# A two-layer network of gated attention and experts: block ends without Pool's drain, the second experts' first inputs prepared in the attention before, and rows gathered by halves

## The chip, the cores and the metric

The kernel runs on one core of a Trainium2 chip. The engines of the core are called TensorE (PE in the rows; its loading of weights is PEld), VectorE (DVE), ScalarE (ACT), Pool (GpSimd) and SyncE (SP), and a q behind an engine's name is the sequencer that reads its instructions. The metric is the device time of one execution in microseconds, as a median of several. The profile is one execution that the hardware profiler took, and its rows count from the start of that execution's span.

## What is computed

Two layers, each a gated cross attention and a gated mixture of experts, on x of 8 x 512 tokens with 256 values. The change touches the seams between the parts, and above all the last part:

```
x = x + tanh(g_xattn[0]) * attention0(layernorm(x), ctx)    # 16 heads, causal
x = x + tanh(g_ffn[0])   * experts0(layernorm(x))           # 32 experts, 8 for each token
x = x + tanh(g_xattn[1]) * attention1(layernorm(x), ctx)    # 16 heads, masked
x = x + tanh(g_ffn[1])   * experts1(layernorm(x))           # 8 experts, 2 for each token
...
E, K, H = (8, 2, 1024)                                      # experts1; T = 4096 tokens
cap = int(K * CAP_FACTOR * ((T + E - 1) // E))              # 1024 places in each expert
logits = xt @ wg
gates_k, idx_k = jax.lax.top_k(softmax(logits), K)          # then divided by their sum
h = jax.nn.relu(jnp.einsum('ecd,edh->ech', disp, w1) + b1[:, None, :])
out = jnp.einsum('ech,ehd->ecd', h, w2) + b2[:, None, :]
y = jnp.einsum('tk,tkd->td', gates_k * valid, out[idx_k, loc_c])
```

Here `disp` holds for each expert the rows of up to 1024 tokens that chose it, in order; places that stay empty give nothing.

## The kernel before

Four stages follow one another, each written as a block in which every engine has its own list of instructions: the first attention, the first experts (`experts0`, 32 experts), the second attention and the second experts (`experts1`, 8 experts). A function `attention` serves both attentions; its tiles belong to an object `Layer`. A block ends at a barrier of all engines. In a block as `nc.Block()` makes it, Pool executes a drain ahead of that barrier (at the line of the function that has the block: 334 in `attention`, 1233 in `experts0`). Behind the block its semaphores are given back: `Semaphores.__exit__` (lines 69 and 70) clears them and adds a barrier of its own. This clearing is built as a second drain of Pool, a clear of the range of semaphores, and then the barrier of line 70.

The second attention works through 8 batches in a software pipeline (`ITERATIONS` from -3 to B + 1). For each batch it ends with the routing: VectorE counts in `base` how many tokens have gone to each expert and makes the places `idx`, and Pool scatters the tokens' rows (the values after the norm, the token's number, the gates) to `rows` in main memory (line 1192). After the last batch VectorE copies the counts to `tot0` (line 1150). SyncE loads and stores around it: `stack` (line 474), the residual `xres` (458), the stores of the new x (488).

`experts1` (line 1490) goes over the 8 experts with `pipeline`: a prologue for expert 0, then one iteration for each expert, `iteration(cur, nxt)`, which also begins the next expert's work. `par` is the expert's parity; most tiles stand twice. Each expert has 1024 rows in 8 tiles of 128:

- Before the first expert VectorE makes the indices of all the experts' rows, `gidx`, from `tot0` in four operations (lines 1638 to 1643: `late`, `gfl`, `gfl`, `gidx`). For each expert `pick` copies its 8 columns to `gidx_e` (1652) and its first bias to `b1_e` (1655); for expert 0 it waits for the biases between the two.
- Pool's `gather` waits for the pick, and for the transposes that last read the buffer `row[par]`, and issues 8 indirect DMAs of 128 rows (1715). They all count up one semaphore for each parity. `add` (1723) issues 8 indirect DMAs that add the finished rows into x.
- TensorE's `turn` (1549 to 1557) transposes four tiles of one half of the columns into the bank `e_x_bank`; four turns make an expert. ScalarE copies the bank to `xT` (1609), and the next turn waits for that copy, since there is one bank. Turn k is column half k // 2 and token half k % 2; turn 0 waits for all 8 gathers.
- `up` (1559 to 1571) is the first product, 16 matmuls for each half of the tokens (block 0 and block 1), into four banks `e_h_bank`, which ScalarE and VectorE empty in turn with bias and relu (1618, 1673). Block 0 waits for the weights and for all four copies of the expert.
- `down` (1575 to 1588) is the second product, four groups of 16 matmuls for a pair of blocks; in block 0 the four turns of the next expert stand behind each 8 of them.
- SyncE loads each expert's `w1` and `w2` (1535, 1536), those of expert 0 at the start of the block, the two biases `b1`, `b2` (1523, 1524) behind the first gathers, and at the end copies x to the output.

Of the kernel before, what the change touches and what calls it, by code (L numbers as in the profile page):

```python
# [13 lines left out]
P = 128  # L14
# [247 lines left out]
class Layer:  # L262


    def __init__(self, c, ctx, layer):
        t_ = lambda name, shape, dt=F32: sb(c, ctx, f"{name}_{layer}", shape, dt)
        sem = lambda n: ctx.enter_context(c.nc.semaphore(f"{n}_{layer}"))
        rows = STACK + (6 if layer == 0 else 3)
# [4 lines left out]
        self.qst = [t_(f"qst{i}", [rows, HEADS, S], BF16) for i in range(2)]  # L273
        self.kst = [t_(f"kst{i}", [rows, HEADS, S], BF16) for i in range(2)]
        self.va = [t_(f"va{i}", [P, NT, HEADS, 32]) for i in range(3)]
        self.m3T = [t_(f"m3T{i}", [3 * HEADS // 2, S], BF16) for i in range(2)]
        if layer:
            self.mask3 = t_("mask3", [P, B * S], BF16)
            self.maskc = t_("maskc", [P, B * NT])
        self.w_in, self.b_in, self.l_in, self.stack_ones, self.w_ones, self.w_t, self.w_put, self.zeroed = (  # L280
# [25 lines left out]
def attention(c, layer, a, x_in, ctx_in, mask, wq, bq, wk, bk, wv, bv, wp, bp, wroute, x_out, rows,  # L306
              qk_dram, mask_dram, tot0=None, token=None):
# [26 lines left out]
    with ExitStack() as ctx:  # L334
# [57 lines left out]
        if layer == 0:  # L392
# [13 lines left out]
                 "hchain", "lo_rdy", "lchain")  # L406
# [5 lines left out]
        block = ctx.enter_context(nc.Block())  # L412
# [33 lines left out]
        def _(sp):  # L446
# [68 lines left out]
            for it in ITERATIONS:  # L515
# [349 lines left out]
        def _(dve):  # L865
# [282 lines left out]
            if tot0 is not None:  # L1148
                dve.wait_ge(evac["rank"], B)
                dve.tensor_copy(tot0[:, :], base[:, 0, :]).then_inc(s["ochain"], 1)  # L1150
# [74 lines left out]
def experts0(c, table, gate_up, down, x, token, a, mask, wq, bq, wk, bk, wv, bv, wp, bp, wroute):  # L1225
# [7 lines left out]
    with ExitStack() as ctx:  # L1233
# [28 lines left out]
        block = ctx.enter_context(nc.Block())  # L1262
# [227 lines left out]
def experts1(c, rows, w1, b1, w2, b2, x, tot0, out):  # L1490
# [4 lines left out]
    with ExitStack() as ctx:  # L1495
        t_ = lambda name, shape, dt=F32: sb(c, ctx, f"e1_{name}", shape, dt)
        two = lambda name, shape, dt=F32: [t_(f"{name}{i}", shape, dt) for i in range(2)]
        names = ("rows_in0", "rows_in1", "weights_in0", "weights_in1", "bias_in", "x_full", "x_evac",
# [3 lines left out]
        rows_in, weights_in = (s["rows_in0"], s["rows_in1"]), (s["weights_in0"], s["weights_in1"])  # L1502
# [3 lines left out]
        h = two("h", [P, HC, HALF])  # L1506
        y = two("y", [P, TILES, D])
        b1_s, b2_s = t_("b1", [P, E1, HC]), t_("b2", [P, E1, D])
        b1_e = two("b1_e", [P, HC])
        gidx = t_("gidx", [P, E1, TILES], U32)  # L1510
        gfl, late = t_("gfl", [P, E1, TILES]), t_("late", [P, E1, TILES])
# [9 lines left out]
        def _(sp):  # L1521
            def biases():
                sp.dma_start(b1_s[:, :, :], b1.rearrange("e (c p) -> p e c", p=P), allow_slow_non_contiguous=True).then_inc(s["bias_in"], 16)
# [257 lines left out]
```

## Time and profile before

| | us |
|---|---|
| median of three runs | 2087.16 (2085.93 to 2091.36) |
| the profiled execution | 2089.91 |
| its span | 2088.2 |
| first attention, in the span | 0 to 652 |
| first experts | 652 to 899 |
| second attention | 899 to 1576 |
| second experts | 1576 to 2072 |
| copy of x to the output | 2072 to 2088 |

The limits of the stages are the barriers, to the nearest microsecond. The rows below are of two kinds. Views such as the busy time or the windows give sums over a stretch; a timeline gives single instructions, or runs of equal ones. In a timeline row the number in brackets is the time for which the engine had stood idle just before, and behind the arrow is what ended that: an engine and its line, a DMA, or "issue", when the profile shows nothing. PEclk is the granted clock of TensorE as a share of 2.4 GHz. The drains are instructions of Pool's sequencer and don't count as busy time of Pool.

### The profile page before, as it was taken

How to read it: one execution, taken by the hardware profiler on the slowest of the kernel's cores; microseconds unless marked ns; L12 is line 12 of the kernel's file. 1: busy time of each engine (PE TensorE's matmuls, PEld its weight loads, DVE VectorE, ACT ScalarE, POOL GpSimd, SP SyncE). 2: the span in 40 equal slices, each digit the busy share in tenths (PEclk: the TensorE clock that was granted, in tenths of full speed). 3: DMA queues.
4: the chain of work that ended last, by engine and by line, in shares of the span. 5: the costliest groups of instructions: out<-in, count | busy, mean ns of one | idle time of the engine just before them, and what ended most of it. 6: DMA issues, size and time to landing. Idle time of an engine off the chain costs nothing. (4 is left out here: it accounts for less than half of the span.)

```text
span 2088.2 us, 29804 instructions
## 1 busy us (share of the span) xinstructions
PE 1779.8 (85%) x10491; PEld 1063.2 (51%) x10491; DVE 1070.1 (51%) x2740; ACT 888.4 (43%) x1684; POOL 605.0 (29%) x580
## 2 busy tenths in 40 slices
PE   3799898989864988737999999999954999999995
PEld 1456555555544877613344444443322666666664
DVE  4556877787745644306877777778321112121121
ACT  3366565655531222222777787766721111111110
POOL 4212211120002777622221233211132233333322
PEclk9999999999976999967999999999976999999998
DMA  3545445334224778625323432431114133333314
GB/s 114 167 121 173 151 137 169 107 121 134 75 74 117 172 164 171 114 75 164 102 67 114 132 119 77 126 110 58 42 47 132 30 78 81 81 76 76 81 20 101
DMA packets 204243, 222.84 MB, mean 107 GB/s; under 512 B 33438, under 2 KB 195231, under 8 KB 203431
## 3 DMA queue, kind: packets, MB, share of 16 engines
q1 hardware_dynamic: 176458, 177.48, 27.7%
q0 software_dynamic: 27648, 43.60, 11.1%
q8 instruction: 78, 1.28, 0.3%
q14 instruction: 59, 0.48, 0.1%
HBM read 155.06 MB, written 86.93 MB: 116 GB/s over the span
## 5 line engine op out<-in xcount | busy, mean ns | idle before, releaser
L889 DVE TENSOR_REDUCE nmx<-mxb 128x1 f32<-128x512 f32 (+1 forms) x896 | 521.7, 608 | 244.0 <-PE mxb L660 147.8
L747 ACT ACTIVATE pt<-stb 128x512 f32<-128x512 f32 x832 | 475.3, 598 | 280.5 <-PE stb L680 155.9
L660 PE MATMUL mxb<-kst,qst 96*128 96x512 bf16 (+4 forms) x1024 | 335.9, 350 | 36.9 <-DVE nmx L889 27.2
L677 PE MATMUL stb<-qst,kst 99*128 99x512 bf16 (+4 forms) x1024 | 327.6, 345 | 8.2 <-DMA qst<-m3T 4.3
L1569 PE MATMUL e_h_bank<-e_xT,e_w 128*128 128x512 f32 x512 | 224.7, 597 | 6.1 <-ACT e_xT L1609 5.4
L1583 PE MATMUL e_y_bank<-e_w,e_h 128*128 128x256 f32 x1024 | 227.0, 379 | 0.0
L693 PE MATMUL ob<-pt,va 128*32 128x512 f32 (+3 forms) x2048 | 220.3, 525 | 2.7 <-ACT pt L747 1.7
L1583 PEld LDWEIGHTS e_y_bank<-e_w,e_h 128*128 128x128 f32 x1024 | 193.0, 190 | 31.7 <-issue 7.2
L677 PEld LDWEIGHTS stb<-qst,kst 102*128 102x128 bf16 (+1 forms) x1024 | 99.5, 99 | 213.3 <-ACT pt L747 136.0
L1171 POOL TENSOR_TENSOR qk<-qk,parts 128x512 f32<-128x512 f32 x64 | 73.0, 1161 | 436.4 <-ACT qk L782 227.8
L1723 POOL DMA_INDIRECT x_after_l<-e_y,e_token x64 | 99.5, 1555 | 282.0 <-DVE e_y L1688 267.3
L660 PEld LDWEIGHTS mxb<-kst,qst 99*128 99x128 bf16 (+1 forms) x1024 | 101.2, 99 | 151.3 <-DVE nmx L889 79.8
L1569 PEld LDWEIGHTS e_h_bank<-e_xT,e_w 128*128 128x128 f32 x512 | 97.3, 191 | 124.8 <-issue 124.2
L1618 ACT ACTIVATE e_h<-e_h_bank,e_b_e 128x512 f32<-128x512 f32 x64 | 44.0, 687 | 269.3 <-PE e_h_bank L1569 269.3
L1673 DVE TENSOR_SCALAR e_h<-e_h_bank,e_b_e 128x512 f32<-128x512 f32 x64 | 48.0, 750 | 171.1 <-PE e_h_bank L1569 171.1
L1684 DVE TENSOR_TENSOR e_y<-e_y_bank,e_b 128x512 f32<-128x512 f32 x32 | 22.1, 691 | 201.8 <-PE e_y_bank L1583 201.8
L1476 POOL DMA_INDIRECT x_after_l<-e_y,token x64 | 102.3, 1598 | 47.5 <-DMA x_after_l<-e_y,token 21.5
L663 PE MATMUL mxb<-hide_max,identb 128*128 128x128 bf16 x512 | 110.9, 223 | 0.0
L680 PE MATMUL stb<-hide_st,identb 128*128 128x128 bf16 x512 | 109.4, 221 | 0.0
L1177 POOL TENSOR_TENSOR parts<-qk,parts 128x512 bf16<-128x512 f32 x64 | 73.0, 1161 | 101.4 <-ACT parts L815 101.4
L1192 POOL DMA_INDIRECT rows<-rowb,idx x64 | 63.8, 997 | 114.3 <-DVE idx L1016 97.2
L1338 PE MATMUL e_bank<-e_xT,e_guT 128*128 128x256 f32 x384 | 88.6, 380 | 2.8 <-DVE e_h L1396 2.8
(242 smaller groups left out, 2514.7 us busy)
## 6 DMA issues: line engine op xcount, KB each, us to landing
qk_parts<-parts SPq DMA_DIRECT2D x16, 1536.0 KB, 6.2
qst<-qk_parts SPq DMA_DIRECT2D x384, 64.0 KB, 2.3
kst<-qk_parts SPq DMA_DIRECT2D x384, 64.0 KB, 2.3
e_w<-in_L_ffn_w SPq DMA_DIRECT2D x16, 1024.0 KB, 7.4
rows<-rows SPq DMA_DIRECT2D x15, 1060.0 KB, 8.7
crow<-in_ctx SPq DMA_DIRECT2D x16, 512.0 KB, 3.9
x_after_l<-xres SPq DMA_DIRECT2D x16, 512.0 KB, 3.3
e_gu_nat<-in_L_ffn_gate_up_proj SPq DMA_DIRECT2D x64, 128.0 KB
```

Source lines behind the costliest of these rows:

```text
L660: last = pe.matmul(out, qst[par][0:rows_used, h, qt * P:(qt + 1) * P], kst[par][0:rows_used, h, 0:nk], start=True, stop=not causal)
L663: last = pe.matmul(out[:, nk - P:nk], c.identb[:, :], c.hide_max[:, :], start=False, stop=True)
L677: last = pe.matmul(bank[:, to:to + S - q_from(kt)], kst[par][0:ROWS, h, kt * P:(kt + 1) * P], qst[par][0:ROWS, h, q_from(kt):S], start=Tru ...
L680: last = pe.matmul(bank[:, to:to + P], c.identb[:, :], c.hide_st[:, :], start=False, stop=True)
L693: last = pe.matmul(ob[32 * j:32 * j + 32, q_from(kt):S], va[b % 3][:, kt, 4 * g + j, :], weights_of(b, g, kt, j), start=kt == 0, stop=kt = ...
L747: act.activation(pt[:, slot(b, u), q0:S], stb[no % N_ST][:, q0:S], ACT.Exp, scale=SCALE).then_inc(s["st_free"], 1)
L889: last = dve.tensor_reduce(nmx[:, qt, h:h + 1], got[:, at:at + k_to(qt)], AX.X, ALU.max, negate=True)
L1338: last = pe.matmul(out, guT[par][:, ci, q, :], xT[par][:, ci, :], start=ci == 0, stop=ci == NC - 1)
L1476: pool.indirect_dma_start(x, bass.IndirectOffsetOnAxis(token[:, TILES * e + i:TILES * e + i + 1], 0), y[e % 3][:, i, :], None, bounds_chec ...
L1569: last = pe.matmul(hb[q % 4][:, :], w1_s[par][:, ci, k * P:(k + 1) * P], xT[par][:, ci, blk * HALF:(blk + 1) * HALF], start=ci == 0, stop= ...
L1583: last = pe.matmul(yb[t][:, i * D:(i + 1) * D], h[blk][:, k, (2 * t + i) * P:(2 * t + i + 1) * P], w2_s[par][:, k, :], start=k == 0, stop= ...
L1723: pool.indirect_dma_start(x, bass.IndirectOffsetOnAxis(token[par][:, i:i + 1], 0), y[par][:, i, :], None, bounds_check=T + SPARE - 1, oob_ ...
```

## The change

*Block ends.* The block of `attention`, and with it both attentions, and that of `experts0` are made with `no_gpsimd_drain=True`. The block of `experts1` stays as it was, and so does `Semaphores.__exit__`.

*Weights and biases.* Tiles of the second attention that are no longer read get a second use: `qst[0]` holds expert 0's `w1` and `w2`, `kst[0]` the biases `b1` and `b2`, and `qst[1]` and `kst[1]` the hidden values `h` of the two blocks. SyncE loads the first four in the attention (a new line 554, in the iteration of the last batch), and waits for them at the end of that block. At the start of `experts1` it loads expert 1's weights, where it loaded expert 0's.

*Indices.* The four operations that make `gidx` stand at the end of VectorE's attention, behind the copy to `tot0`.

*Halves.* The gathers of an expert count up two semaphores, one for each four tiles. Turn k is now column half k % 2 and token half k // 2, and each pair of turns waits for its own four gathers. Block 0 of `up` waits for two copies, block 1 for four. In the prologue two turns and block 0 of `up` stand ahead of the other two turns. ScalarE's and VectorE's lists follow: ScalarE copies twice, empties block 0's banks and copies twice more; VectorE's `gates`, which needs all 8 gathers, stands behind its part of block 0.

The diff, cut to its core:

```diff
-        block = ctx.enter_context(nc.Block())
+        block = ctx.enter_context(nc.Block(no_gpsimd_drain=True))
...
+                if ffn and cur == B - 1:
+                    sp.wait_ge(s["st_full"], N_SCORE * (B - 1))
+                    for src, dst in zip(ffn, (a.w1, a.w2, a.b1, a.b2)):
+                        sp.dma_start(dst, src, allow_slow_non_contiguous=True).then_inc(s["ffn_in"], 16)
...
+            if ffn:
+                sp.wait_ge(s["ffn_in"], 64)
             sp.wait_ge(s["x_out"], 16 * B)
...
-        w1_s, w2_s = two("w1", [P, NC, F1]), two("w2", [P, HC, D])
+        w1_s, w2_s = [a.w1, t_("w1", [P, NC, F1])], [a.w2, t_("w2", [P, HC, D])]
...
             def first(n):
-                load(n)
-                sp.wait_ge(rows_in[0], 16 * TILES)
-                biases()
+                pass
...
             def turn(n, k):
-                par, cc, hf = n[1], k // 2, k % 2
-                if k == 0:
-                    pe.wait_ge(rows_in[par], n[0] * (16 * TILES) + 16 * TILES)
+                par, cc, hf = n[1], k % 2, k // 2
+                if cc == 0:
+                    pe.wait_ge(rows_in[par][hf], n[0] * HALF_IN + HALF_IN)
...
                 if k0 == 0 and blk == 0:
-                    pe.wait_ge(weights_in[par], b[0] * 32 + 32)
-                    pe.wait_ge(s["x_evac"], at(4, b, 4))
+                    wait(pe, weights_in[par], b[0] * 32 + 32 * par)
+                if k0 == 0:
+                    pe.wait_ge(s["x_evac"], at(4, b, 2 * blk + 2))
...
             def prologue(n):
-                for k in range(4):
+                for k in range(2):
                     turn(n, k)
                 up(n, 0, 0, HC)
+                for k in range(2, 4):
+                    turn(n, k)
...
-                                            bounds_check=2 * SLOTS - 1, oob_is_err=True).then_inc(rows_in[par], 16)
+                                            bounds_check=2 * SLOTS - 1, oob_is_err=True).then_inc(rows_in[par][2 * i // TILES], 16)
```

How the order of instructions moves is shown at three places. The first is TensorE at the start of `experts1`, before: `e_row` are the gathered rows, `e_x_bank` the transposes' bank, `e_h_bank` and `e_y_bank` the banks of the first and the second product.

```order
L1556 MATMUL e_x_bank<-ident,e_row 128x128 x16
L1569 MATMUL e_h_bank<-e_xT,e_w 128x512 x32
L1583 MATMUL e_y_bank<-e_w,e_h 128x256 x8
L1556 MATMUL e_x_bank<-ident,e_row 128x128 x4
L1583 MATMUL e_y_bank<-e_w,e_h 128x256 x8
L1556 MATMUL e_x_bank<-ident,e_row 128x128 x4
L1583 MATMUL e_y_bank<-e_w,e_h 128x256 x8
```

And now, where `qst_1` is the attention's tile that holds expert 0's weights and the hidden values:

```order
L1571 MATMUL e_x_bank<-ident,e_row 128x128 x8
L1585 MATMUL e_h_bank<-e_xT,qst_1 128x512 x16
L1571 MATMUL e_x_bank<-ident,e_row 128x128 x8
L1585 MATMUL e_h_bank<-e_xT,qst_1 128x512 x16
L1599 MATMUL e_y_bank<-qst_1 128x256 x8
L1571 MATMUL e_x_bank<-ident,e_row 128x128 x4
L1599 MATMUL e_y_bank<-qst_1 128x256 x8
L1571 MATMUL e_x_bank<-ident,e_row 128x128 x4
```

Of the 16 transposes that stood ahead of all matmuls, 8 have moved between block 0 and block 1 of the first product; the alternation with the second product, from there on, is as it was.

The second place is SyncE from the end of the second attention into `experts1`, before: `x_after_l` is x in main memory, `e_w` and `e_b` the tiles of weights and biases.

```order
L488 DMA x_after_l<-xres 128x4x256
L458 DMA xres<-x_after_l 128x4x256
L488 DMA x_after_l<-xres 128x4x256
L334 UNCONDITIONAL_BRANCH
L1520 UNCONDITIONAL_BRANCH
L1535 DMA e_w<-in_L_ffn_w 128x2x1024
L1536 DMA e_w<-in_L_ffn_w 128x8x256
L1523 DMA e_b<-in_L_ffn_b 128x64x1
L1524 DMA e_b<-in_L_ffn_b 128x2048
L1535 DMA e_w<-in_L_ffn_w 128x2x1024
L1536 DMA e_w<-in_L_ffn_w 128x8x256
```

And now:

```order
L495 DMA x_after_l<-xres 128x4x256
L465 DMA xres<-x_after_l 128x4x256
L554 DMA qst_1<-in_L_ffn_w 128x2x1024
L554 DMA qst_1<-in_L_ffn_w 128x8x256
L554 DMA kst_1<-in_L_ffn_b 128x64x1
L554 DMA kst_1<-in_L_ffn_b 128x2048
L495 DMA x_after_l<-xres 128x4x256
L341 UNCONDITIONAL_BRANCH
L1541 UNCONDITIONAL_BRANCH
L1550 DMA e_w<-in_L_ffn_w 128x2x1024
L1551 DMA e_w<-in_L_ffn_w 128x8x256
```

Expert 0's weights and the biases have moved ahead of the last store of the attention, and expert 1's weights stand where expert 0's stood.

The third is VectorE at the same seam, before: `tot` are the counts, `slot_in` and `slot_at` constant tables.

```order
L1150 COPY tot<-base 128x8
L334 UNCONDITIONAL_BRANCH
L1634 UNCONDITIONAL_BRANCH
L1638 TENSOR_TENSOR e_late<-slot_in,tot 128x64
L1639 TENSOR_SCALAR e_gfl<-tot 128x64
L1641 TENSOR_TENSOR e_gfl<-e_gfl,e_late 128x64
L1643 TENSOR_TENSOR e_gidx<-e_gfl,slot_at 128x64
L1652 COPY e_gidx_e<-e_gidx 128x8
L1655 COPY e_b_e<-e_b 128x8
L1662 CAST e_token<-e_row 128x8
```

And now:

```order
L1163 COPY tot<-base 128x8
L1166 TENSOR_TENSOR late<-slot_in,tot 128x64
L1167 TENSOR_SCALAR gfl<-tot 128x64
L1169 TENSOR_TENSOR gfl<-gfl,late 128x64
L1171 TENSOR_TENSOR gidx<-gfl,slot_at 128x64
L341 UNCONDITIONAL_BRANCH
L1654 UNCONDITIONAL_BRANCH
L1664 COPY e_gidx_e<-gidx 128x8
L1665 COPY e_b_e<-kst_1 128x8
L1684 TENSOR_SCALAR qst_1<-e_h_bank,e_b_e 128x512 x4
```

The four operations on the indices have moved ahead of the block's end, so that the pick of expert 0's indices, `e_gidx_e`, is the first that VectorE does in `experts1`.

## Rows read from the trace of the kernel before

**Rows 1.** Section 1 of the page: busy time, share of the span, instructions.

```profile
PE 1779.8 (85%) x10491; PEld 1063.2 (51%) x10491; DVE 1070.1 (51%) x2740; ACT 888.4 (43%) x1684; POOL 605.0 (29%) x580
```

**Rows 2.** TensorE timeline, 1589 to 1700: start, us, line, operation, count, [idle before].

```profile
1590.23 1.12 PE L1556 MATMUL e_x_bank<-ident,e_row 128*128 128x128 f32 x4 [35.44 <-DMA e_row<-rows,e_gidx_e]
...
1593.84 1.11 PE L1556 MATMUL e_x_bank<-ident,e_row 128*128 128x128 f32 x4 [0.69 <-ACT e_xT L1609]
...
1597.53 29.45 PE L1569 MATMUL e_h_bank<-e_xT,e_w 128*128 128x512 f32 x64 [0.78 <-ACT e_xT L1609]
...
1643.28 13.97 PE L1569 MATMUL e_h_bank<-e_xT,e_w 128*128 128x512 f32 x32 [0.73 <-issue]
```

**Rows 3.** Timeline of Pool, 1540 to 1605.

```profile
1577.98 1.10 POOL L1715 DMA_INDIRECT e_row<-rows,e_gidx_e  x1 [10.29 <-DVE e_gidx_e L1652]
...
1582.04 1.01 POOL L1715 DMA_INDIRECT e_row<-rows,e_gidx_e  x1 [0.30 <-issue]
...
1587.30 1.01 POOL L1715 DMA_INDIRECT e_row<-rows,e_gidx_e  x1 [0.31 <-issue]
```

**Rows 4.** Timeline of VectorE, 1540 to 1605.

```profile
1576.09 0.23 DVE L1638 TENSOR_TENSOR e_late<-slot_in,tot 128x64 f32<-128x64 f32 x1 [19.10 <-PEq L70]
...
1576.97 0.17 DVE L1652 COPY e_gidx_e<-e_gidx 128x8 uint32<-128x8 uint32 x1
```

**Rows 5.** Gathers issued in 1577 to 1579, then in 1581.8 to 1583.

```profile
DMA to landing us min/median/max: 6.3/6.3/6.3
...
DMA to landing us min/median/max: 3.4/3.4/3.4
```

**Rows 6.** Lines 334, 1233, 69: instruction, count, ns least/median/most, from to; idle.

```profile
L334 POOLq DRAIN  x2: 306/2795/5284, 622.9 to 1569.6; - x2
...
L1233 POOLq DRAIN  x1: 4137/4137/4137, 895.0 to 895.0; - x1
...
L69 POOLq DRAIN  x3: 98/173/174, 651.6 to 1575.0; - x3
```

**Rows 7.** Timeline of TensorE, 1655 to 2075.

```profile
1689.48 3.62 PE L1583 MATMUL e_y_bank<-e_w,e_h 128*128 128x256 f32 x16
1692.94 0.60 PE L1556 MATMUL e_x_bank<-ident,e_row 128*128 128x128 f32 x4
...
1700.72 0.60 PE L1556 MATMUL e_x_bank<-ident,e_row 128*128 128x128 f32 x4
1702.09 14.00 PE L1569 MATMUL e_h_bank<-e_xT,e_w 128*128 128x512 f32 x32 [0.76 <-ACT e_xT L1609]
...
1743.47 3.62 PE L1583 MATMUL e_y_bank<-e_w,e_h 128*128 128x256 f32 x16
1747.79 0.66 PE L1556 MATMUL e_x_bank<-ident,e_row 128*128 128x128 f32 x4 [0.71 <-DMA e_row<-rows,e_gidx_e]
1748.29 3.62 PE L1583 MATMUL e_y_bank<-e_w,e_h 128*128 128x256 f32 x16
```

**Rows 8.** Waits of TensorE, 1605 to 2030: us in sum, count, us of one.

```profile
PE e_h_bank L1569 <- ACT e_xT L1609: 4.6, 6, 0.8
PE e_x_bank L1556 <- DMA e_row<-rows,e_gidx_e: 4.4, 6, 0.8
```

**Rows 9.** Windows: us, busy PE, PEld, DVE, ACT, POOL; clock, DMA share, GB/s.

```profile
1508.00:1539.00 31.00, 25.80 (x177) 12.75 (x173) 7.73 (x43) 17.24 (x34) 7.89 (x8) 0.94 0.15 53
...
1597.00:1601.00 4.00, 3.47 (x4) 1.52 (x5) 0.38 (x3) 0.39 (x1) 0.00 (x0) 0.50 0.99 393
...
1997.00:2065.00 68.00, 68.00 (x255) 48.08 (x253) 12.54 (x23) 5.50 (x8) 18.45 (x12) 1.00 0.20 23
```

**Rows 10.** Timeline of SyncE, 1475 to 1600.

```profile
1507.90 0.37 SPq L458 DMA_DIRECT2D xres<-x_after_l  x1
1539.06 0.36 SPq L488 DMA_DIRECT2D x_after_l<-xres  x1
...
1590.61 4.68 SPq L1524 DMA_DIRECT2D e_b<-in_L_ffn_b  x1
```

More of the change, by code:

```diff
@@ L272, in __init__ @@
         self.wr = t_("wr", [P, NC, (E0, E1)[layer]])
-        self.qst = [t_(f"qst{i}", [rows, HEADS, S], BF16) for i in range(2)]
-        self.kst = [t_(f"kst{i}", [rows, HEADS, S], BF16) for i in range(2)]
+        self.qst = [t_(f"qst{i}", [P, HEADS, S], BF16) for i in range(2)]
+        self.kst = [t_(f"kst{i}", [P, HEADS, S], BF16) for i in range(2)]
         self.va = [t_(f"va{i}", [P, NT, HEADS, 32]) for i in range(3)]
@@ L1486, in _, with experts1 @@
                 pool.wait_ge(added[i], 16 * TILES * (E0 // 2))
-def experts1(c, rows, w1, b1, w2, b2, x, tot0, out):
+def experts1(c, a, rows, w1, w2, x, out):
     nc = c.nc
@@ L1620, in prologue @@
             def prologue(n):
-                for k in range(4):
+                for k in range(2):
                     evac(n, k)
                 hidden(n, 0, (0, 2, 4, 6))
+                for k in range(2, 4):
+                    evac(n, k)
             def iteration(cur, nxt):
@@ L1635, in _, with pick @@
         def _(dve):
-            full = tot0[:, :].unsqueeze(2).to_broadcast([P, E1, TILES])
-            dve.tensor_tensor(late[:, :, :], c.slot_in[:, :, :], full, ALU.is_ge).then_inc(s["ichain"], 1)
-            dve.tensor_scalar(gfl[:, :, :], full, -1.0, float(SLOTS), ALU.mult, ALU.add).then_inc(s["ichain"], 1)
-            dve.wait_ge(s["ichain"], 2)
-            dve.tensor_tensor(gfl[:, :, :], gfl[:, :, :], late[:, :, :], ALU.mult).then_inc(s["ichain"], 1)
-            dve.wait_ge(s["ichain"], 3)
-            dve.tensor_tensor(gidx[:, :, :], gfl[:, :, :], c.slot_at[:, :, :], ALU.add).then_inc(s["ichain"], 1)
-            dve.wait_ge(s["ichain"], 4)
-            def pick(n, first=False):
+            def pick(n):
                 par = n[1]
                 e = n[0] * 2 + n[1]
-                wait(dve, s["rows_in" + str(par)], n[0] * (16 * TILES))
+                for half in rows_in[par]:
+                    wait(dve, half, n[0] * HALF_IN)
                 wait(dve, s["act_h"], at(8, n, -8))
                 dve.tensor_copy(gidx_e[par][:, :].unsqueeze(1), gidx[:, bass.ds(e, 1), :]).then_inc(s["picked"], 1)
-                if first:
-                    dve.wait_ge(s["bias_in"], 32)
                 dve.tensor_copy(b1_e[par][:, :].unsqueeze(1), b1_s[:, bass.ds(e, 1), :]).then_inc(s["small"], 1)
@@ L1659, in gates @@
                 e = n[0] * 2 + n[1]
-                dve.wait_ge(rows_in[par], n[0] * (16 * TILES) + 16 * TILES)
+                for half in rows_in[par]:
+                    dve.wait_ge(half, n[0] * HALF_IN + HALF_IN)
                 wait(dve, s["added"], at(16 * TILES, n, -16 * TILES))
@@ L1690, in prologue @@
             def prologue(n):
-                pick(n, True)
+                pick(n)
+                hidden(n, 0, (1, 3, 5, 7))
                 gates(n)
-                hidden(n, 0, (1, 3, 5, 7))
             def iteration(cur, nxt):
```

50 lines of the change are left out of this document (32 added, 18 removed).

## The prediction

> **What bounds the kernel now.** I read the busy shares first: TensorE is busy for 85% of the span, no other engine for more than 51% [rows 1]. A mean over unlike stages prices nothing, so I went to the stretch that the change touches, the end of the second attention and the second experts, about 1557 to 2088 us, a quarter of the time.
>
> At its start TensorE stands for 35.44 us: its last work of the attention ends at 1554.79 (1590.23 less 35.44), the first transposes of the experts begin at 1590.23, and the row names the gathered rows as what ended the wait [rows 2]. Pool's and VectorE's timelines divide this hole: VectorE gets going at 1576.09, after a barrier [rows 4]; Pool issues the first gather at 1577.98, the fourth at 1582.04, the eighth and last at 1587.30 [rows 3]. What stands before the barrier are Pool's drains: the one that ends the attention starts at 1569.6 and takes 5.284 us, that of the first experts 4.137 us [rows 6].
>
> Behind the hole TensorE is the bound: from 1997 to 2065 it is busy 68.00 of 68 us at a granted clock of 1.00, that is 2.4 GHz [rows 9]. Before that it stops twice in each round: six waits on the gathered rows, 4.4 us in sum, and six on ScalarE's copy of the transposed rows, 4.6 us [rows 8]. One round is 58.81 us (1689.48 to 1748.29) [rows 7].
>
> **The change, part by part.**
>
> *Indices.* Four VectorE operations stood between the barrier and the pick of the first indices, from 1576.09 to 1576.97 [rows 4]: 0.88 us on the path, since Pool waits for that pick. They now follow the copy of the counts, which ends VectorE's attention at 1556.99 (1576.09 less 19.10 of idle) [rows 4], while the block ends with Pool at 1574.9 (1569.6 + 5.284) [rows 6]. Some 18 us cover them; without cover they would cost the 0.88 again.
>
> *Gathers by halves.* TensorE needs only the first four gathers to begin. The fourth started at 1582.04 and landed 3.4 us later [rows 3, 5], so at 1585.44, against 1590.23 for all eight: 4.79 us. Issued 0.88 earlier it gains 5.67 if the landing moves too. But the first gather took 6.3 us to land where the fourth took 3.4 [rows 5]: both land right behind the weight loads that SP issues at the same moment, and it still issues as many bytes there, now those of expert 1. I take 5.2, between the ends 4.79 and 5.67. The other four gathers now lie beside the first half's matmuls; these take over 13 us [rows 7], the gathers 5.3 us (1582.04 to 1587.30) and a landing.
>
> *Transposes.* Before the first large matmul stood four groups of transposes, each with ScalarE's copy behind it; now two. The latter two cost 3.69 us there (1593.84 to 1597.53), at half clock [rows 2]. They come back between the two runs of matmuls, at full clock: 0.60 us of matmuls [rows 7] and 0.69 of waiting for the copy [rows 2], twice, 2.6 us. Gain 1.1, and 0 if the clock is still low there. It was granted at 0.50 until about 1601, some 3.5 us into the dense matmuls [rows 9], so it should be up; I take 1.0. The half-speed stretch itself is neither gained nor lost: it follows the start of dense work, which only comes earlier.
>
> *The two waits of a round.* The first half is awaited alone at the first transposes, and it was issued 5.3 us earlier than the last gather, for a wait of 0.71 [rows 7]: the wait goes. Transposes now go by halves of the tokens, so a new expert's first matmuls need the first two copies, done some 7 us before, and not the fourth: this wait goes too. Prices are taken start to start, since a wait also breaks the overlap of neighbouring matmuls. Rows: from the second product's group at 1743.47 to the transposes at 1747.79 are 4.32 us, against 3.46 without a wait (1689.48 to 1692.94), so 0.86. Copy: from the last transposes at 1700.72 to the matmuls at 1702.09 are 1.37, against 0.50 (1747.79 to 1748.29), so 0.87 [rows 7]. Six rounds have the first, seven changes of expert the second: 5.2 + 6.1 = 11.3 us. By the idle times alone it would be 9.7 (4.4 + 4.6, and the 0.73 of the first change, which is listed as issue) [rows 2, 8]. What is late next is TensorE itself; the gathers' first half has over 4 us to spare.
>
> *Weights and biases in the attention.* Four loads join SP's queue behind the last load of the residual, 1507.90, and ahead of the last store, 1539.06; nothing of SP lies between [rows 10]. Issuing them takes some 6 us, of which the broadcast of a bias 4.68 [rows 10]. Their 3.1 MB need 8 us at the 393 GB/s of 1597 to 1601, and the DMA engines have a share of 0.15 from 1508 to 1539 [rows 9]. Nothing in the experts waited for the first expert's weights, so nothing is gained either: 0. Were the cover gone, the last store would slip, and only the block's end waits for that.
>
> *Ends without a drain.* Pool's drain ahead of the barrier goes at two places that matter, 5.284 and 4.137 us [rows 6]. But the semaphores are still cleared behind the barrier, and that begins with a drain of Pool (line 69), and all engines wait for it at the next barrier. Today it takes 98 to 174 ns [rows 6], because the other has just been paid. The drain's length follows from what Pool did before: 306 ns behind plain arithmetic, 4 to 5 us behind indirect DMAs [rows 6]. So the second drain should take over the wait of the first. Ends: 0, and 9.4 us if the time belongs to the removed instruction. I take 0.2 us a place for the short drain that merges, 0.4.
>
> The Trainium skill ("Perfetto Trace Analysis", section "Sequencer-only Instruction (DRAIN, etc)") lists a drain as sequencer work with two actors, the sequencer and the semaphores. By that the time would go with the instruction, which is the first rival below. The rows speak against it with a spread of 306 to 5284 ns.
>
> **Sum.** 5.2 + 1.0 + 11.3 + 0.4 = 17.9 us (the 0.88 is inside the 5.2). The profiled execution took 2089.91 us, 2.75 above the median of 2087.16, and becomes 2072.0; the median becomes **2069.3**.
>
> **Rivals.**
> - *The drains really go.* The rest as above and 9.0 us more (9.4 less the 0.4 counted): 2060.3. For it: the drain at line 69 has never been seen paying. Against it: 306 ns where no DMA stood before. Chance 0.12.
> - *Another wait takes the place of the two in the round*, say the banks of the first product, so that a round stays at 58.8 us: only 6.6 remain, 2080.6. Against it: where rows came early, at the first change, TensorE ran on without any row wait. Chance 0.06.
> - *The halves do not do what they say*: the fourth gather is held behind expert 1's weights until the eighth is nearly there. Then 5.2 shrinks to nothing: 2074.5. Against it the 3.4 us. Chance 0.03.
> - *Slower: the clock falls.* With both gaps gone TensorE streams through the loop, some 400 us, and if the clock were then granted at 1.2 GHz for part of it, each us at that level gives half a us back. It decides from 36 us on; 50 us would give 2094. Against it: 68 us without any gap at 1.00 [rows 9]. Chance 0.02.
> - The forecast itself: 0.77.
>
> **How the numbers follow.** The forecast's own span: the least gain is 4.8 + 0 + 9.7 + 0 = 14.5 (2072.7), the most 5.7 + 1.1 + 12.0 + 0.6 = 19.4 (2067.8), where 12.0 and 0.6 add a tenth of a us to each of the thirteen waits and to each barrier; with two us for the scatter of single runs 2066 to 2075. The drains' case must lie inside to keep what is left out under 2 in 10, so the range is 2058 to 2075. A measurement of this kernel tells 0.3% from no change, 6.3 us: faster means below 2080.9. Forecast, drains, halves and half of the second rival: 0.95 faster, 0.03 the same, 0.02 slower.
>
> **What would show it.** Right: TensorE's hole of 35.4 us becomes about 30; two groups of transposes, 16 matmuls, two groups, 16 matmuls; the list of waits for TensorE in the loop is nearly empty, a round is about 57 us; line 69's drain takes 4 to 5 us. Drains gone: it stays at 0.17 and VectorE starts the second experts near 1570.7. Wrong: a round still near 58.8, a granted clock under 1.00 in the loop, or a first half that lands later than 1585.5 counted from the same barrier.

## The result, and the profile after

The changed kernel takes 2055.18 us (four runs, 2052.29 to 2058.18) beside 2086.55 for the kernel before (four runs): a ratio of 0.9862, with a 95% interval of 0.9843 to 0.9882. The forecast of 2069.3 promised a gain of 18 us and the range ended at 2058; the gain is 31 us in this comparison, and two more comparisons further down give 0.9860 and 0.9885. The direction was right, the size was not. Line numbers below are those of the kernel that is named; the changed one has 1571, 1585 and 1599 where the kernel before has 1556, 1569 and 1583.

The first view is the timeline of TensorE in the changed kernel from 1540 to 1620, the answer to [rows 2] (start, us, line, operation, count, idle before and what ended it):

```profile
1570.52 1.11 PE L1571 MATMUL e_x_bank<-ident,e_row 128*128 128x128 f32 x4 [26.21 <-DMA e_row<-rows,e_gidx_e]
...
1574.12 16.82 PE L1585 MATMUL e_h_bank<-e_xT,qst 128*128 128x512 f32 x32 [0.69 <-ACT e_xT L1627]
1590.78 0.60 PE L1571 MATMUL e_x_bank<-ident,e_row 128*128 128x128 f32 x4
...
1593.41 14.00 PE L1585 MATMUL e_h_bank<-e_xT,qst 128*128 128x512 f32 x32 [0.69 <-ACT e_xT L1627]
1607.24 3.62 PE L1599 MATMUL e_y_bank<-qst 128*128 128x256 f32 x16
```

The hole ahead of the first transposes is 26.21 us, where it was 35.44, and the prediction said about 30. Behind it stand two groups of transposes, 32 matmul records (16 matmuls; each is recorded twice, as before), two groups, 32 records: the order that was forecast. TensorE's list of waits from 1605 to 2000 is empty, where [rows 8] had twelve. The rounds are seen in the timeline from 1655 to 1725, the answer to [rows 7]:

```profile
1664.09 3.62 PE L1599 MATMUL e_y_bank<-e_w,qst 128*128 128x256 f32 x16
1667.55 0.60 PE L1571 MATMUL e_x_bank<-ident,e_row 128*128 128x128 f32 x4
1667.98 3.62 PE L1599 MATMUL e_y_bank<-e_w,qst 128*128 128x256 f32 x16
...
1679.22 0.60 PE L1571 MATMUL e_x_bank<-ident,e_row 128*128 128x128 f32 x4
1679.66 13.90 PE L1585 MATMUL e_h_bank<-e_xT,qst 128*128 128x512 f32 x32
1693.40 13.98 PE L1599 MATMUL e_y_bank<-e_w,kst 128*128 128x256 f32 x64
...
1720.94 3.62 PE L1599 MATMUL e_y_bank<-qst 128*128 128x256 f32 x16
```

A round is 56.85 us (1664.09 to 1720.94) instead of 58.81. No transposes wait for rows and no matmuls for a copy. Two windows of the changed kernel (us, busy of PE, PEld, DVE, ACT and POOL with counts, granted clock, DMA share, GB/s), the answer to [rows 9]:

```profile
1577.00:1581.00 4.00, 4.00 (x8) 1.67 (x7) 0.24 (x1) 0.69 (x1) 0.00 (x0) 0.65 0.00 0
...
1600.00:2030.00 430.00, 430.00 (x1589) 291.32 (x1588) 87.58 (x178) 56.57 (x86) 146.81 (x113) 1.00 0.30 64
```

From 1600 to 2030 the granted clock was 1.00 and TensorE busy throughout, so the rival by which the clock falls did not happen. The first of the two is spoken of below.

The drains of Pool's lines 69 and 70, the answer to [rows 6] (instruction, count, ns least, median and most, first and last start):

```profile
L69 POOLq DRAIN  x3: 88/172/182, 650.9 to 1559.2; - x3
...
L70 POOLq DRAIN  x3: 39/43/51, 651.6 to 1560.0; - x3
```

Here the prediction fell. With the drain at the block's end gone, that of line 69 takes 88 to 182 ns, as it did before (98 to 174), and nothing else takes the time over. Pool's timeline, the answer to [rows 3], shows the way from its last scatter to its gathers:

```profile
1556.24 0.97 POOL L1213 DMA_INDIRECT rows<-rowb,idx  x1 [0.30 <-issue]
1561.28 1.10 POOL L1726 DMA_INDIRECT e_row<-rows,e_gidx_e  x1 [4.07 <-DVE e_gidx_e L1664]
...
1565.33 1.01 POOL L1726 DMA_INDIRECT e_row<-rows,e_gidx_e  x1 [0.30 <-issue]
```

From the end of the last scatter's issue to the first gather are 4.07 us. Before, the idle time in the same place was 10.29 [rows 3].

### The profile page after: what moved, and what is told of

The parts are those of the page before. It is cut to its first block and busy times, and to the rows that moved or that the text cites. A ratio compares the mean times of both kernels' runs of the same rounds, so it can differ in the third digit from the quotient of the medians.

```text
span 2056.1 us, 29834 instructions
## 1 busy us (share of the span) xinstructions
PE 1774.4 (86%) x10491; PEld 1061.7 (52%) x10491; DVE 1069.3 (52%) x2740; ACT 888.6 (43%) x1684; POOL 603.5 (29%) x580
## 5 line engine op out<-in xcount | busy, mean ns | idle before, releaser
L1695 DVE TENSOR_TENSOR e_y<-e_y_bank,kst 128x512 f32<-128x512 f32 x32 | 22.1, 692 | 196.1 <-PE e_y_bank L1599 196.1
L1585 PE MATMUL e_h_bank<-e_xT,qst 128*128 128x512 f32 x256 | 114.2, 605 | 1.4 <-ACT e_xT L1627 1.4
L1585 PE MATMUL e_h_bank<-e_xT,e_w 128*128 128x512 f32 x256 | 111.2, 592 | 0.0
L1636 ACT ACTIVATE kst<-e_h_bank,e_b_e 128x512 f32<-128x512 f32 x32 | 22.0, 687 | 183.9 <-PE e_h_bank L1585 183.9
L706 PEld LDWEIGHTS ob<-pt,va 128*32 128x32 f32 x2048 | 45.9, 109 | 77.6 <-issue 59.1
L1488 POOL DMA_INDIRECT e_row<-table,token x64 | 68.1, 1065 | 49.7 <-issue 49.4
L590 PE MATMUL work<-ident,xn 128*128 128x128 f32 x128 | 23.5, 322 | 67.9 <-ACT xn L808 60.4
```

What stands on the lines that cost most here:

```text
L706: last = pe.matmul(ob[32 * j:32 * j + 32, q_from(kt):S], va[b % 3][:, kt, 4 * g + j, :], weights_of(b, g, kt, j), start=kt == 0, stop=kt = ...
L1585: last = pe.matmul(hb[q % 4][:, :], w1_s[par][:, ci, k * P:(k + 1) * P], xT[par][:, ci, blk * HALF:(blk + 1) * HALF], start=ci == 0, stop= ...
```

## Where the time went, stretch by stretch

The two traces differ by 32.1 us. The table cuts each trace at the same events, read from timelines as above: the end of issue of the last scatter of the first experts, VectorE's first operation in the second attention, the end of issue of the last scatter there, the first gather, the first transposes, the first matmuls of the second product (L1583 before), and the end of issue of the last scatter of all. It holds the traces of all kernels that were run; the next section tells what they are.

| kernel | to last scatter of first experts | seam 1 | second attention | seam 2 | gather to transposes | to second product | to last scatter | rest |
|---|---|---|---|---|---|---|---|---|
| before | 892.48 | 7.57 | 667.64 | 10.29 | 12.25 | 36.59 | 443.80 | 17.58 |
| before_again | 883.37 | 7.42 | 663.27 | 10.48 | 12.14 | 36.33 | 443.61 | 17.78 |
| changed | 888.94 | 3.47 | 664.80 | 4.07 | 9.24 | 36.72 | 431.01 | 17.85 |
| after_again | 888.59 | 3.35 | 664.59 | 4.17 | 9.26 | 35.78 | 431.01 | 17.65 |
| after_third | 892.64 | 3.39 | 663.29 | 4.17 | 9.27 | 36.78 | 431.00 | 17.76 |
| drain_only | 885.98 | 3.38 | 662.52 | 5.34 | 12.21 | 37.10 | 443.74 | 17.53 |
| drain_only_2 | 888.39 | 3.37 | 665.50 | 5.00 | 12.18 | 37.58 | 443.94 | 17.34 |
| drains_kept | 887.10 | 7.51 | 662.93 | 9.46 | 8.50 | 36.07 | 431.00 | 17.43 |
| no_halves | 893.10 | 3.31 | 663.35 | 4.23 | 12.24 | 37.56 | 444.04 | 17.77 |
| rows_all | 889.12 | 3.42 | 667.47 | 4.10 | 12.27 | 35.81 | 437.13 | 17.48 |
| held | 887.78 | 3.36 | 667.38 | 4.27 | 6.92 | 36.85 | 431.01 | 17.93 |
| early_held | 884.30 | 3.26 | 666.46 | 2.88 | 6.98 | 35.31 | 431.01 | 18.00 |
| probe | 890.77 | 7.43 | 666.55 | 9.43 | 9.44 | 35.62 | 431.02 | 21.74 |

The stretches that the change touches repeat within about 0.3 us between traces of one kernel, but for the one to the second product: there TensorE starts at half speed, and the moment at which its granted clock rises varies. The two long ones, whose code is the same but for some loads and indices, do not repeat: the two traces of the kernel before differ by 9.1 and 4.4 us there, 13.5 in sum, half of what the whole change gives. The granted clock differs with them: from 75 to 100 us behind the start of the second attention it was 0.70 in the first of these two traces and 0.93 in the second. Of the 45 executions of the kernel before that ran beside the experiments, the ten of up to 2080 us had a mean clock of 0.945 to 0.949 and the four of over 2090 us one of 0.938 to 0.940; whether the clock makes the time or follows it no run here shows. So the touched columns are where the change is read: 4.1 at seam 1, 6.2 at seam 2, 2.9 to the transposes, nothing that these traces show from there to the second product, 12.7 in the loop (means of the two and the three traces). With the rest the columns from seam 1 on, without the second attention, come to 528.1 and 527.8 us before and 502.4, 501.2 and 502.4 after: **25.9 us**, against the 17.9 of the prediction.

## The experiments

**The whole once more, and the drains by themselves.** Four kernels on one chip beside the kernel before: the changed one again, the kernel before with only the blocks' ends edited, the changed one with the drains put back, and one with drains written by hand.

drain_only is the kernel before with this edit at the blocks of `attention` and `experts0`, and drains_kept the changed kernel with the reverse edit:

```diff
-        block = ctx.enter_context(nc.Block())
+        block = ctx.enter_context(nc.Block(no_gpsimd_drain=True))
```

> The changed kernel once more, to separate what the change does from what differs between single executions. The two traces differ by 32.1 us; the places that the change touches account for 25.8 of it (4.1 and 5.3 us where the drains stood, 4.0 from the first gather's issue to the first transposes and the indices, 12.4 from there to the end), and 6.3 us lie in stretches whose code is the same: the experts up to their last scatter (2.8), the second attention (2.8), the first attention (0.7). Theory 1: those 6.3 are scatter between executions, and then the gain over five rounds is about 26 us (ratio 0.9875) and the three stretches vary by 2 to 3 us between executions of the same kernel. Rival: they belong to the change, the gain is 31 to 32 us (ratio 0.985), and the three stretches come out short again.

> The kernel before with one edit: the blocks of both attentions and of the first experts end without Pool's drain. Theory 1 (the time belongs to that drain, and nobody takes it over): 4.1 + 5.3 = 9.4 us less, about 2077 against 2086.5, ratio 0.9955, and the drain at line 69 stays under 0.2 us. The prediction's theory (the next drain pays): 0.4 us less, ratio 1.000, and line 69 takes 4 to 5 us. A third, that leaving the drain out also shortens the scatters and loads of the following stage: 15 us less, ratio 0.993.

> The changed kernel with the drains put back; everything else of the change stays. Theory 1: 9.4 us slower than the changed kernel, so a gain of 16 to 17 us over the kernel before (ratio 0.992), with drains of about 4.1 and 5.3 us in the trace. The prediction's theory: as fast as the changed kernel within 0.5 us. If the sum has another gain that the prediction missed and that isn't a drain, this kernel keeps it: 20 us or more.

Measured: after_again 2057.28 us beside 2087.75, ratio 0.9860 (0.9835 to 0.9885); drain_only 2072.20, ratio 0.9934 (0.9909 to 0.9958); drains_kept 2069.68, ratio 0.9917 (0.9892 to 0.9941). In the trace of drain_only the seams are 4.2 and 5.0 us shorter than before, and line 69 is still quick:

```profile
L69 POOLq DRAIN  x3: 93/167/168, 645.1 to 1554.3; - x3
```

The prediction's theory, by which drain_only gains 0.4 us and drains_kept loses nothing to the changed kernel, is out by all of these. Of theory 1 the place is right: 9.1 us are gone at the seams (9.3 by the means of both traces of each kernel). In drains_kept the two drains are back, with 4.137 and 5.284 us, and its touched columns come to 510.0 us, 17.9 below the kernel before; the prediction's sum without its term for the drains was 17.5. The sizes by the medians stayed open, since 15 us and 12 us are more than 9, as 30 is more than 26. So the changed kernel and drain_only were run again, on another chip.

> The changed kernel once more, on the chip of this call, for a second ratio beside the kernel before. The places that the change touches have given 26.2 us by every trace so far (4.1 and 6.2 at the seams, 3.0 for the gathers, 0.2 to 0.7 for the transposes, 12.8 in the loop), while the medians of the runs lay 29 to 31 us apart. Theory 1 (26 us, the rest is scatter): ratio 0.9875, interval about the same width as before. Rival (another 4 us belong to the change, in stretches that it leaves alone): 0.9855 again.

> The kernel before without the drains alone, once more, on the chip of this call. The seams of its trace are 4.2 and 5.0 us shorter, 9.2 us, but the medians were 15 us apart. Theory 1 (the rest is scatter of the stretches between, which differed by up to 8 us between traces of the same kernel): about 9 us here, ratio 0.9955. Rival (leaving the drains out shortens what follows as well): 14 us again, ratio 0.993.

Measured: after_third 2059.05 us beside 2082.86, ratio 0.9885 (0.9867 to 0.9903); drain_only_2 2078.53, ratio 0.9966 (0.9948 to 0.9984), by which the gain is 7 us (4.3 by the medians). The rivals' 0.9855 and 0.993 lie outside these intervals. The 25.9 us of the touched columns are a ratio of 0.9876, which lies inside the intervals of all three comparisons of the changed kernel, and the 9.3 us of the drains, 0.9955, inside both of drain_only: the runs tell no excess from noise. Runs of the kernel before lay between 2076 and 2094 us, so a median of six runs says little about 4 us, and the touched columns say more. Nor do the traces have an excess in the long stretches: these two come to 1553.5 us on the mean of the four traces with plain drains at the seams and to 1553.8 in the nine without; to 1552.3 in the four of the kernel before with or without its drains and to 1554.4 in the nine others. The second trace of the kernel before was taken to see this scatter.

> The kernel before once more, for a second trace of it. In the first pair of traces 6 us of the difference lay in stretches whose code the change leaves alone. If that is scatter between executions, the stretch up to the last scatter of the first experts (892.5 us in the first trace) and the second attention from the barrier to its last scatter (667.6 us) come out otherwise here by some us, while the stretches at the two seams and in the second experts repeat within 0.2 us: 7.57 and 10.29 us at the seams, 12.25 from the first gather to the first transposes, 443.8 from the first group of the second product to the last scatter. If the 6 us belong to the change, both long stretches repeat, 892 and 667 to 668.

before_again was one execution, of 2076.14 us. The long stretches came out at 883.4 and 663.3 us, the touched ones as expected within 0.2.

**What the drain waits for.** The probe puts drains by hand into the changed kernel:

```diff
+            pool.drain()
+            pool.drain()
...
+                pool.memset(pad[:, :], 0.0)
+                pool.drain()
...
             pool.wait_ge(s["added"], 16 * TILES * E1)
+            pool.wait_ge(s["copied"], 16)
```

The first pair stands at the end of the first experts, the second edit at the end of Pool's list in the second attention, the third ahead of the last block's own drain.

> What a plain drain of Pool waits for. The changed kernel with drains written by hand: two in a row at the end of the first experts, directly behind the wait for the last scatter; at the end of each attention one behind a clearing of a tile of 8 columns; and at the end of the second experts Pool waits for the copy of x to the output (over 10 us) ahead of the block's own drain. Theory a (what is left of the indirect DMAs has to finish, though their landings have been seen): the first takes 4 us, the second next to nothing, the one behind the small operation still 4 to 5 us, the one behind 10 us of idling next to nothing. Theory b (a fixed price of the first plain drain behind indirect DMAs): 4, nothing, 4 to 5, and 4 us also behind the idling, which then lengthens the run by 4 us. Theory c (an ordinary operation in between pays or clears it): 4, nothing, 0.3 us or the operation itself takes 4, and 4 us at the end.

The four drains, in rows of the probe's lines (1511 and 1512 the pair, 1245 behind the memset, 1521 the last block's), and then the last block's drain in the changed kernel, where Pool does not wait for the copy (line 1516):

```profile
L1511 POOLq DRAIN  x1: 4133/4133/4133, 893.1 to 893.1; - x1
...
L1512 POOLq DRAIN  x1: 40/40/40, 897.3 to 897.3; - x1
...
L1245 POOLq DRAIN  x1: 5407/5407/5407, 1566.5 to 1566.5; - x1
...
L1521 POOLq DRAIN  x1: 4307/4307/4307, 2067.4 to 2067.4; - x1
```

```profile
L1516 POOLq DRAIN  x1: 4309/4309/4309, 2040.6 to 2040.6; - x1
```

This is theory b: 4.1 us for the first, 0.04 for the second, 5.4 behind the small operation, and 4.3 at the end, 17 us behind the last scatter's issue and with the copy to the output done in between; the rest of the run is 21.7 us there instead of 17.8. In the changed kernel the same drain starts 2.4 us behind the end of the last scatter's issue (2038.25) and takes 4.309 us, against 4.307 in the probe: the 15 us more of waiting took nothing off it. All scatters had landed long before, so what is paid there is not a transfer that still runs. In the probe the price is paid by the first plain drain behind indirect DMAs, early or late. It is not the same everywhere: 4.1 us behind the first experts, 5.3 to 5.4 behind the second attention, 4.0 to 4.3 at the last block. Why line 69's drain does not pay it is not settled. In the built program it differs by a range of semaphores that it carries, and behind it the plain drain of line 70 is short as well (39 to 51 ns), though it is the first plain one behind the scatters of the changed kernel. Line 69 also stands behind a barrier, where the slow drains stand ahead of one; no run puts a plain drain there, so that the form of the drain decides, and not its place, is not shown.

**The halves.** no_halves takes them back in the changed kernel, rows_all only the split wait for the rows:

```diff
-                par, cc, hf = n[1], k % 2, k // 2
-                if cc == 0:
-                    pe.wait_ge(rows_in[par][hf], n[0] * HALF_IN + HALF_IN)
+                par, cc, hf = n[1], k // 2, k % 2
+                if k == 0:
+                    for half in rows_in[par]:
+                        pe.wait_ge(half, n[0] * HALF_IN + HALF_IN)
...
-                if k0 == 0:
-                    pe.wait_ge(s["x_evac"], at(4, b, 2 * blk + 2))
+                if k0 == 0 and blk == 0:
+                    pe.wait_ge(s["x_evac"], at(4, b, 4))
```

and the prologues of TensorE and ScalarE with four turns ahead of block 0. In rows_all only the wait for the rows is edited; the order of the turns, the wait for the copies and the prologues stay as changed.

> The changed kernel with the halves undone: the first transposes of an expert wait for all eight gathers, the turns go by column halves first, block 0 of the first product waits for all four copies, and the prologue has its four turns ahead of block 0. Drains, indices and weights stay as changed. By the traces the halves are worth 3.0 us from the gather to the first transposes, nothing from there to the second product, and 12.8 us in the loop: 15.8 us slower than the changed kernel, 2072.7. By the prediction's terms: 4.3 + 1.0 + 11.3 = 16.6 us, 2073.5. Rival (the loop's gain comes from elsewhere, from the weights that are loaded earlier or from tiles at other places): under 8 us slower.

> The changed kernel with one of the two waits of a round back: the first transposes of an expert wait for all eight gathers, while the turns still go by token halves. The prediction's split: the wait on the rows costs 0.86 us in each of six rounds, and the first transposes come as late as without halves, 12.25 us after the first gather instead of 9.25: 5.2 + 3.0 = 8.2 us slower than the changed kernel, 2065.1. Rival 1 (the waits cover one another, the gain needs both): most of the 15.8 us come back, 2071. Rival 2 (the order of the turns is what counts, the rows come early enough): 3 us slower, 2060.

Measured: no_halves 2074.69 us beside 2082.33, ratio 0.9959 (0.9941 to 0.9978); rows_all 2069.91, ratio 0.9934 (0.9912 to 0.9956). By the table the touched stretches of no_halves come to 519.2 us, 17.2 above the mean of the changed kernel's 502.0, where the prediction's terms gave 16.6 and the first pair of traces 15.8: 3.0 lie ahead of the transposes, 13.0 in the loop and 1.1 between. Those of rows_all come to 510.2, 8.2 more, as expected and neither rival: 3.0 ahead of the transposes, 6.1 in the loop, the rest scatter. In its timeline (1655 to 1735) the wait for the rows is back and that for the copy is not:

```profile
1669.04 3.62 PE L1600 MATMUL e_y_bank<-e_w,qst 128*128 128x256 f32 x16
1673.54 0.65 PE L1572 MATMUL e_x_bank<-ident,e_row 128*128 128x128 f32 x4 [0.89 <-DMA e_row<-rows,e_gidx_e]
...
1685.27 0.60 PE L1572 MATMUL e_x_bank<-ident,e_row 128*128 128x128 f32 x4
1685.71 13.90 PE L1586 MATMUL e_h_bank<-e_xT,qst 128*128 128x512 f32 x32
```

So the wait for the rows costs 6.1 us by itself (437.13 less 431.01), with no wait for the copies beside it. The 6.7 us to the kernels without halves (443.8, the mean of their five traces, less 437.13) are left for the copies; no run puts that wait back alone.

**The gathers behind the weights.**

```diff
             def first(n):
-                pass
+                sp.wait_ge(rows_in[0][0], HALF_IN)
```

> The changed kernel, with SyncE holding back the load of expert 1's weights until the first four gathers of expert 0 have landed. In the changed kernel the fourth gather lands 5.1 us after its issue, where the last ones take 2.7 to 2.9. Theory 1 (the gathers stand behind 2.1 MB of weights that SyncE issues 1 us earlier): all of them land in about 2.9 us, the way from the first gather's issue to the first transposes falls from 9.25 to about 7.0, and the run gains 2.2 us on the changed kernel (2054.7 against 2056.9). Rival (the first gathers are slow by themselves): 9.2 us stays, gain 0. Expert 1's weights then arrive near 17 us after the barrier and are needed 60 us after it, so nothing waits for them.

Measured: 2056.17 us beside 2082.33, ratio 0.9866 (0.9836 to 0.9896). The time alone doesn't tell it from the changed kernel, the trace does. The times from issue to landing (least, median, most), first of the gathers that held issues from 1562 to 1569, the first five, then of the changed kernel's fourth gather:

```profile
DMA to landing us min/median/max: 2.8/2.8/2.9
```

```profile
DMA to landing us min/median/max: 5.1/5.1/5.1
```

The first gather and the first transposes of held:

```profile
1562.79 1.10 POOL L1726 DMA_INDIRECT e_row<-rows,e_gidx_e  x1 [4.27 <-DVE e_gidx_e L1664]
```

```profile
1569.71 1.11 PE L1571 MATMUL e_x_bank<-ident,e_row 128*128 128x128 f32 x4 [24.08 <-DMA e_row<-rows,e_gidx_e]
```

With the weights held the first transposes come 6.92 us behind the first gather instead of 9.25: theory 1, and 2.3 us of the hole were the weights.

**Further on the same path.** The first four gathers are issued in the attention:

```diff
+                pool.wait_ge(s["ichain"], 6)
+                for i in range(CAP1 // P // 2):
+                    pool.indirect_dma_start(a.row0[:, i, :], None, rows, bass.IndirectOffsetOnAxis(a.gidx0[:, i:i + 1], 0),
+                                            bounds_check=2 * SLOTS - 1, oob_is_err=True).then_inc(a.rows0[2 * i // (CAP1 // P)], 16)
...
-            pipeline(pool, E1, gather, iteration)
+            pipeline(pool, E1, lambda n: gather(n, TILES // 2), iteration)
```

> A version that goes further on the same path: Pool issues the first four gathers of expert 0 in the second attention, as soon as its own last scatter has landed and ahead of the barrier (rows into a tile of the attention that is free by then, the biases into the tile of the mask), and SyncE holds expert 1's weights until these have landed. From the last scatter to the first transposes the changed kernel takes 13.3 us (4.1 to the first gather, 9.25 from there), the version with held weights alone 11.2. Theory (the barrier's 2.2 us between the last landing and the first gather go, and a gather lands in 2.9): 1.9 + 6.9 = 8.8 us, 4.5 less than the changed kernel. The barrier then comes some 5.3 us later, since Pool issues four gathers ahead of it, about 7 us behind the last scatter, still ahead of the landing. Rival (the later barrier ends last): first transposes at 9 to 11 us, a gain of 2 to 4.

Measured: 2052.01 us beside 2082.86, ratio 0.9859 (0.9840 to 0.9878), on the chip on which the changed kernel had 0.9885. It has the lowest median of all; the two intervals overlap, so that it beats the changed kernel too is read from the trace. Pool's timeline from 1550 to 1572, and then TensorE's:

```profile
1553.05 0.97 POOL L1218 DMA_INDIRECT rows<-rowb,idx  x1 [0.31 <-issue]
1556.90 1.10 POOL L1250 DMA_INDIRECT kst<-rows,gidx  x1 [2.88 <-issue]
...
1560.96 1.01 POOL L1250 DMA_INDIRECT kst<-rows,gidx  x1 [0.31 <-issue]
```

```profile
1563.88 1.12 PE L1580 MATMUL e_x_bank<-ident,kst 128*128 128x128 f32 x4 [22.75 <-DMA kst<-rows,gidx]
```

From the last scatter's end (1554.02) to the first transposes are 9.86 us, where the changed kernel takes 13.3: 3.4 us less, and 1.1 more than the theory's 8.8. The size lies in the rival's range, but the mechanism is not the rival's: the barrier ended near 1563.5, ahead of the fourth landing, which ended TensorE's wait. The first gather started 2.9 us behind the scatter instead of 1.9. The drain of line 69 is long in this kernel:

```profile
L69 POOLq DRAIN  x3: 87/182/3704, 644.4 to 1558.5; - x3
```

Started at 1558.5 while Pool was at its four gathers, it lasted 3.70 us, until 0.2 us after the last of them had been issued (1561.97). It ended ahead of the landing at 1563.9, so it did not wait for that. As far as one row can show, it waited for Pool to finish issuing.

## Why the prediction came out wrong, step by step

- *Indices*, 0.88 us: right. drains_kept has them moved and the drains in place, and its seam 2 is 9.46 us against 10.29 and 10.48.
- *Gathers by halves*, 5.2 with the indices in it: 3.9 (0.9 and 2.9). The term took the landing of the fourth gather as 3.4 us [rows 5]; it was 5.1. Counted from the barrier the fourth landed after 10.2 us (1570.4 less 1560.25) instead of 9.4 (1585.44 less 1576.05), one of the signs of being wrong that the prediction named. The index operations had kept the gathers 1.93 us behind SyncE's weight load (1576.05 to 1577.98), without them they follow 1.03 us behind (1560.25 to 1561.28), and held shows that the weights are in their way. The prediction named this in a rival and weighed it at its full size only, not in part. Part of it stays open: with the drains kept, at the same distance of 1.04 us, the fourth gather landed in 4.4 us, and the way to the first transposes was 0.7 us shorter (8.50 against 9.25).
- *Transposes*, 1.0: about 0.9, by all the traces together. The kernel before and the changed one do not show it: from the first transposes to the second product they take 36.6 and 36.3 us before, 36.7, 35.8 and 36.8 after. What hides it is the moment at which the granted clock rises from 0.50. In the first trace of the kernel before it came 3.5 us into the first matmuls [rows 9]. In the changed kernel the clock was 0.65 on the mean from 1577 to 1581, so it rose near 1579.8, 5.7 us into them. This delay varies whatever the kernel: 3.0 to 5.7 us in the five traces with four groups of transposes ahead of the first matmuls, 2.8 to 6.0 in the eight with two, 4.5 on the mean of either. The stretch takes 37.0 us on the mean of the five and 36.1 on that of the eight.
- *The two waits of a round*, 11.3: 12.7 to 12.8. The mechanism was right and the size a tenth of a us low at each of the thirteen waits on the mean; the parts were 5.2 and 6.1 in the forecast, 6.1 and 6.7 in rows_all. A tenth more at each of them, the prediction's own widest case, is 12.6 and not the 12.0 that it wrote. The row taken as free of a wait for the copy, 0.50 us [rows 7], had itself a longer record of transposes (0.66 instead of 0.60): without a wait it is 0.44 (1679.22 to 1679.66), and the matmuls behind a wait took 0.09 longer as well (13.83 against 13.74 start to start).
- *Weights and biases*, 0: right, with another size. The two bias loads alone kept SyncE for 12.2 us, where some 6 had been counted for all four loads; the last store came 30.95 us behind the last load of the residual (31.16 before [rows 10]), and nothing waited.
- *Ends without a drain*, 0.4: 9.3 in drain_only, and this is **the step that failed**: "So the second drain should take over the wait of the first." The premise, that the length follows from what Pool did before, fits the four plain drains of the probe. The conclusion needed more: that the drain of line 69 is the same thing as that of the block's end. Its rows of 98 to 174 ns were read as those of a drain whose price had been paid, and no row showed it unpaid. The forecast rested on that for the largest unknown of the sum, and gave 0.12 to the case that came true. What the runs showed in its place: with the block's drain gone line 69's still takes 0.17 us, and 9.3 us go at the two seams. Why the one drain costs 4 to 5 us and the other 0.17 stays open.

The Trainium skill ("Perfetto Trace Analysis", section "Sequencer-only Instruction (DRAIN, etc)") has two actors in a drain, the sequencer and the propagation of semaphores. That the time went with the removed instruction, 9.3 us in drain_only, is in line with it; the section has no price for either drain.

Without the drains the forecast was 17.5 us, and the other terms came to 16.6, or to 17.5 with the transposes by all the traces. That this part of the sum fits so well is partly luck: the gathers, 1.3 too high, and the waits, 1.4 too low, cancel.

With the drains' rival (2060.3) the forecast would have been 1 us off the 2061.3 that the touched stretches give (2087.16 less 25.9). The first four runs lie at 2055, 6 us further down and below the range. That is put down to scatter, since the interval of their ratio holds the 25.9 us and the long stretches of the traces show no gain; the range had allowed 2 us for it, where single executions of the kernel before spread over 18.

## What to carry to other kernels

A drain of Pool at a block's end was a price of its own at all three places where indirect DMAs ran before it, and it shows in the time only where all engines wait at the barrier: 4.1 and 5.3 us at two seams, none at the last block, where the copy to the output covers it. When a removed instruction has a second one of the same name behind it, put the two cases at even chances unless a row shows the second one unpaid, and let the range reach both. And where an operation is taken out ahead of a DMA, look at which other transfer the DMA then moves up to.

## What the runs showed of the hardware that was not expected

- A plain drain of Pool behind indirect DMAs, with no other drain between, took 4.0 to 5.4 us: 4.309 us when it came 2.4 us behind the last scatter's issue, 4.307 when it came 17 us behind it. A second one right behind it took 0.04 us.
- The drain that goes with the clearing of semaphores took 0.09 to 0.19 us behind the same scatters, with or without another drain ahead of it, and 3.70 us in the one kernel in which Pool was still issuing gathers.
- A gather of 128 rows landed 2.8 to 2.9 us after its issue when no load of weights had been issued shortly before it, and the first four took 4.4 to 6.5 us when 2 MB of weights had been issued 1 us ahead of them.
